# One block for the second and third feed-forward stage, the first head pair prepared early, and masks made in the first attention

## What is computed

```python
x = x + L0_xattn(layernorm(x), ctx)            # 16 heads of 16
x = x + L0_ffn(layernorm(x), w_gate, w_up, w_down)
x = x + L1_xattn(layernorm(x), ctx, mask, ...)  # 16 heads of 64, a null key and value
x = x + L1_ffn(layernorm(x), ...)              # 8 experts, the best two
```

```python
x = act_qdq(x)                      # scale = max|x| / 32767
up = act_qdq(x @ deq(w_up).T)
gate = act_qdq(x @ deq(w_gate).T)
sig = fixed_qdq_u16(sigmoid(gate))
gate = act_qdq(gate * sig)
o = act_qdq(gate * up)
return o @ deq(w_down).T
```

## Time and profile before

| what | value |
|---|---|
| median of three executions | 1203.74 us (1201.26 to 1206.43) |
| the profiled execution | 1201.73 us, span 1200.0 us |
| PE busy | 1092.3 us, 91% |
| DVE busy | 954.8 us, 80% |
| ACT busy | 602.0 us, 50% |
| POOL busy | 473.6 us, 39% |
| stage 2 of the feed-forward step | 384.2 to 482.0 |
| stage 3 | 482.0 to 566.9 |
| stage 4 | 566.9 to 644.7 |

### The profile page before, as it was taken

How to read it: one execution, slowest core, us unless ns; L and a number is a source line. 1 busy time by engine, 2 the same in 40 slices (tenths; PEclk the granted TensorE clock), 3 DMA queues, 4 the chain that set the end, 5 groups by cost and what they waited for, 6 DMA issues and landing times. The chain is left out here.

```text
span 1200.0 us, 19905 instructions
## 1 busy us (share of the span) xinstructions
PE 1092.3 (91%) x6208; PEld 902.4 (75%) x6208; DVE 954.8 (80%) x2563; ACT 602.0 (50%) x1337; POOL 473.6 (39%) x546
## 2 busy tenths in 40 slices
PE   7899999996898885895997899999999969999997
PEld 5677777885786664442996898889989858888786
DVE  4688998886685989897664888988888759888886
ACT  1566766773555887586781333433433323333332
POOL 1245445432000757674000444555554434343433
PEclk9899999998899998687898999999999979999999
DMA  9000000000233686597204011011000000000000
GB/s 275 1 2 1 1 1 1 1 2 1 106 119 127 220 291 245 162 350 266 88 1 144 21 44 45 1 45 45 1 1 1 1 1 19 18 17 17 26 18 26
DMA packets 50048, 82.56 MB, mean 69 GB/s; under 512 B 4636, under 2 KB 35696, under 8 KB 49968
## 3 DMA queue, kind: packets, MB, share of 16 engines
q1 hardware_dynamic: 48591, 80.77, 19.9%
q10 hardware_dynamic: 1376, 0.79, 0.3%
HBM read 45.65 MB, written 35.90 MB: 68 GB/s over the span
## 5 line engine op out<-in xcount | busy, mean ns | idle before, releaser
L1134 PE MATMUL a_ps<-VW,a_PT 128*128 128x256 f32 x640 | 143.5, 379 | 0.0
L1134 PEld LDWEIGHTS a_ps<-VW,a_PT 128*128 128x128 f32 x640 | 120.2, 190 | 15.0
L1172 ACT ACTIVATE a_U<-a_U 128x1280 f32<-128x1280 f32 x32 | 40.7, 1271 | 110.7 <-DVE a_U L1257 110.7
L2245 POOL TENSOR_TENSOR m_half<-m_half 128x512 f32<-128x512 f32 x32 | 41.2, 1286 | 130.6 <-ACT m_half L2207 130.6
L1151 ACT COPY a_PT<-a_ps 128x512 f32<-128x512 f32 (+1 forms) x96 | 46.0, 517 | 82.6 <-PE a_ps L1097 82.6
L2147 PE MATMUL m_ps<-m_wh,m_xh 128*128 128x512 f32 x256 | 86.6, 420 | 0.0
L915 DVE TENSOR_SCALAR a_U<-a_ps 128x320 f32<-128x320 f32 x128 | 59.2, 484 | 32.8 <-PE a_ps L723 21.5
L1850 POOL TENSOR_SCALAR f_sg<-f_sg 128x1024 f32<-128x1024 f32 x24 | 36.7, 1529 | 113.6 <-ACT f_sg L1807 113.2
L2147 PE MATMUL m_ps<-m_wl,m_xh 128*128 128x512 f32 x256 | 80.9, 398 | 0.0
L1249 DVE TENSOR_REDUCE a_mx<-a_ps 128x4 f32<-128x320 f32 x128 | 62.4, 488 | 22.8 <-PE a_ps L1084 22.4
L2147 PE MATMUL m_ps<-m_wh,m_xl 128*128 128x512 f32 x256 | 80.6, 396 | 0.0
(11 more groups left out here) (257 smaller groups left out, 3179.6 us busy)
## 6 DMA issues: line engine op xcount, KB each, us to landing
up_scratch<-f_ub SPq DMA_DIRECT2D x24, 512.0 KB, 3.0
f_ul<-up_scratch SPq DMA_DIRECT2D x24, 512.0 KB, 5.5
key_scratch<-p_keys SPq DMA_DIRECT2D x8, 640.0 KB, 6.7
vw_scratch<-p_vw SPq DMA_DIRECT2D x16, 320.0 KB, 5.7
k_raw<-key_scratch SPq DMA_DIRECT2D x8, 640.0 KB, 6.1
VW<-vw_scratch SPq DMA_DIRECT2D x4, 1280.0 KB, 5.7
xs<-in_x SPq DMA_DIRECT2D x4, 1024.0 KB, 12.4
h_scratch<-f_hh SPq DMA_DIRECT2D x8, 512.0 KB, 2.7
```

What stands on the lines that cost most here:

```text
L1134: last = pe.matmul(Y[:, 0:D], PTs[t.p][:, j, :], fold.values[t.batch % 2][:, j, :], start=(j == 0), stop=(j == NJ - 1))
```

## The change

- The blocks of stages 2 and 3 become one. On each engine the third stage's work follows the second's without a common end in between; the necessary waits are written out (ACT waits for `s_ua`, `s_uw` and `s_sc` before the first `ints`, POOL for `kup` alone).
- The first head pair is prepared at the end of stage 2: `mask_key(0)` in DVE's last chunk, then `mask_key(1)` and `mask_value(0)` ahead of the two maxima; on PE two query transposes, two key products, a value product and the four folded keys of pair 0 ahead of `rows_max(2)`. In stage 3 pair m now goes with units 3m-3 to 3m-1, and an iteration m = 8 has only units and the values of pair 7.
- `rows_max`, `fold_max`, `spread_max` and `integer_scale` use a list of banks `top`, and the column `2 * P` for the spread value. The last one lies in a bank that the value products do not use, and its wait for `s_We` is gone.
- `masks` moves to the first attention, behind body t = 28 on DVE (`MASKS = 28`), with its loads on SP behind the loads of x; the masks are stored to `mask_scratch` and read back as two contiguous tiles in `load_small`, which has six transfers instead of seven.
- The null value is no longer added from a tile of its own; POOL copies it to column `NKEY` of each sequence.
- `load_values` and `load_out` of the first two pairs leave chunks 2 and 3 and come between the first loads of up units behind the last store. The weight tiles are placed in other parts of the freed weights, so they can't be loaded before the last up product.

```diff
 class Prepare0:
+    def masks(self, dve):
+        dve.wait_ge(self.s_mk, 48)
+        dve.memset(mb[:], 0.0).then_inc(s_nv, 1)
+        dve.wait_ge(s_nv, 1)
+        dve.tensor_copy(mb[:, :, 0:NKEY], self.m8[:, :, 0:NKEY]).then_inc(s_nv, 1)
+        dve.wait_ge(s_nv, 2)
+        dve.tensor_scalar(nm[:], mb[:], -1.0, 1.0, ALU.mult, ALU.add).then_inc(s_nv, 1)
+        dve.tensor_reduce(nneg[:], mb[:, :, 0:NKEY], AX.X, ALU.add).then_inc(s_nv, 1)
+        dve.wait_ge(s_nv, 4)
+        dve.tensor_scalar(nm[:], nm[:], self.nk[:, 0:1], None, ALU.mult).then_inc(s_nv, 1)
+        dve.tensor_scalar(nneg[:], nneg[:], float(-NKEY), None, ALU.add).then_inc(s_nv, 1)
...
 # attention0, vector
+                    if t == MASKS:
+                        pr.masks(dve)
...
 # null_value, gpsimd
-        pool.tensor_tensor(self.VT[m % 2][:], self.VT[m % 2][:], self.nve[:].rearrange("p b k -> p (b k)"),
-                           ALU.add).then_inc(self.s_ve, 1)
+        pool.tensor_copy(self.VT[m % 2][:].rearrange("p (b k) -> p b k", b=B)[:, :, NKEY],
+                         self.nv[:, 0:1].broadcast_to([P, B])).then_inc(self.s_ve, 1)
...
 # ffn
+        top = [ps[6], ps[7], ps[6], ps[7], ps[0]]
...
 # tensor, behind the up products
+                pe.wait_ge(s_ue, MF * NCH)
+                p1.query_T(pe, 0, 0)
+                p1.query_T(pe, 0, 1)
+                p1.key_product(pe, 0)
+                p1.key_product(pe, 1)
+                p1.value_product(pe, 0)
+                folded(0)
                 rows_max(pe, 2)
                 rows_max(pe, 3)
                 spread_max(pe, 2)
                 spread_max(pe, 3)
+                for m in range(1, NM):
+                    p1.value_product(pe, m)
+                    if m + 1 < NM:
+                        p1.key_product(pe, m + 1)
+                    folded(m)
+                p1.folded_value(pe, NM - 1, 0)
+                p1.folded_value(pe, NM - 1, 1)
+                rows_max(pe, 4)
+                spread_max(pe, 4)
...
 # scalar
+                act.wait_ge(s_g2, NU)
+                for i in range(4):
+                    p1.key_out(act, 0, i)
...
+                act.wait_ge(s_sc, SCALED)
+                ints(0)
+                ints(1)
+                for m in range(1, NM + 1):
+                    if m < NM:
+                        p1.key_out(act, m, 0)
+                        p1.key_out(act, m, 1)
+                    ints(3 * m - 1)
+                    p1.value_out(act, m - 1, 0)
...
 # sync
                     if t.t0 in (2, 3):
                         p1.load_keys(sp, t.t0 - 2)
-                        p1.load_values(sp, t.t0 - 2)
-                        p1.load_out(sp, t.t0 - 2)
...
-                for i in range(4):
-                    load(sp, At(i))
+                p1.load_values(sp, 0)
+                load(sp, At(0))
+                p1.load_out(sp, 0)
+                load(sp, At(1))
+                p1.load_values(sp, 1)
+                load(sp, At(2))
+                p1.load_out(sp, 1)
+                load(sp, At(3))
+                p1.load_values(sp, 2)
+                p1.store_keys(sp, 0)
...
 # vector
+                        if t.t0 == NCH - 1 and q == 1:
+                            p1.mask_key(dve, 0)
                 pipeline(dve, body, 0, NCH - 1, 2, 5)
+                p1.mask_key(dve, 1)
+                p1.mask_value(dve, 0)
...
-                product(0)
-                p1.masks(dve)
-                p1.mask_key(dve, 0)
-                for m in range(NM):
-                    if m >= 1:
-                        product(3 * m)
-                    p1.mask_value(dve, m)
-                    product(3 * m + 1)
+                for m in range(1, NM + 1):
+                    product(3 * m - 3)
+                    if m < NM:
+                        p1.mask_value(dve, m)
+                    product(3 * m - 2)
                     if m + 1 < NM:
                         p1.mask_key(dve, m + 1)
-                    product(3 * m + 2)
+                    product(3 * m - 1)
```

More of the change, by code:

```diff
@@ L540, in query_T @@
             pe.wait_ge(self.s_wk[0], 32)
[L541 to L542 removed]
+        last = pe.transpose(self.query_bank(m, k), self.wq[m // 2 % 2][:, k, m % 2 * P:(m % 2 + 1) * P],
+                            self.ident[:])
         if m == 0:
@@ L1506, in ffn @@
     ROUND = 12582912.0
+    SCALED = 16
     def s(n):
@@ L1815, in _, with ints @@
                 pipeline(act, body, 0, NCH - 1, 2, 5)
+                p1.key_scale(act)
+                for k in range(KT):
+                    act.wait_ge(p1.s_T, k + 1)
+                    p1.query_out(act, 0, k)
+                act.wait_ge(s_g2, NU)
+                for i in range(4):
+                    p1.key_out(act, 0, i)
+                def ints(u):
+                    if u >= NU:
+                        return
+                    if u >= 2:
+                        act.wait_ge(s_pr, u - 1)
+                    act.activation(gq[u % 2][:], unit(u), ACT.Copy, scale=ksl).then_inc(s_g3, 1)
+                act.wait_ge(s_ua, NU)
+                for i in range(2):
+                    act.wait_ge(s_uw[i], 16 * NU // 2)
+                act.wait_ge(s_sc, SCALED)
[8 more added lines that the diff above has]
+                    if m < NM:
+                        p1.key_out(act, m, 2)
+                    ints(3 * m)
+                    if m < NM:
+                        p1.key_out(act, m, 3)
+                    p1.value_out(act, m - 1, 1)
+                    ints(3 * m + 1)
             @block.sync
@@ L1855, in _, with rounded @@
                     body(At(t))
+                def rounded(u):
+                    if u < NU:
+                        v = ul[u % 4][:]
+                        pool.wait_ge(s_ul[u % 4], 16 * (u // 4 + 1))
+                        pool.tensor_scalar(v, v, kup, ROUND, ALU.mult, ALU.add).then_inc(s_uq, 1)
+                p1.null_key(pool, 0)
+                p1.null_value(pool, 0)
+                p1.null_key(pool, 1)
+                pool.wait_ge(s_sc, SCALED - 4)
+                rounded(0)
+                rounded(1)
+                for m in range(1, NM + 1):
+                    rounded(3 * m - 1)
+                    if m < NM:
+                        p1.null_value(pool, m)
+                    rounded(3 * m)
+                    if m + 1 < NM:
+                        p1.null_key(pool, m + 1)
+                    rounded(3 * m + 1)
             @block.vector
```

239 lines of the change are left out of this document (86 added, 153 removed).

## The result

The changed kernel takes 1195.84 us (median of 20 runs, 1190.64 to 1204.79) where the kernel before takes 1204.72 on the same chip (20 runs, 1198.98 to 1210.26): a ratio of 0.9927, 95% interval 0.9910 to 0.9945, or 8.9 us less. The profiled execution of the changed kernel took 1196.02 us (span 1194.3), 5.7 less than that of before. So the forecast of 1196.8 holds for the total. Its parts don't all: two costs and one gain were taken too small, and another gain has the wrong cause.

What follows compares the result with a forecast made beforehand. It took DVE as the busiest engine that cannot overlap itself in stages 2 and 3. The terms +1.6 - 3.3 + 2.0 - 3.1 - 4.1 gave -6.9 us, a median of 1196.8 us, own range 1193.5 to 1200.

Steps and rivals of the forecast that it cites:

- part 3: Seam between stages 2 and 3: pair 0's work ahead of the maxima delays product 0, +2.0 us (+0.4 to +3.7).
- part 4: Stage 3 itself: DVE loses the mask work (1.9 us) and three of sixteen pair masks (1.2 us), -3.1 us.
- part 1: First attention: six mask instructions on DVE behind body t = 28 push the next clip, +1.6 us (0 to 2.3).
- The first attention's end at 298.6: Sign expected in the profile after: the first attention ends 1.6 us later, at 298.6.
- Part 2: Stage 2: fewer loads on SP ahead of the stores shorten DVE's three stalls, -3.3 us (0 to 5.2 gained).
- Rival (a): Stage 2's stores are limited by bytes, so fewer loads bring about 0: -3.6 in all, 1200.1 us; chance 16%.
- the slow end: Seam with PE at 1.2 GHz: folded keys end near 483.6, product 0 starts at 487.8, +3.7 us.
- rival (c): Stage 3: DVE's stalls on ACT go as well, up to -5.4 us, 1191.4 us; chance 16%.
- Part 5: Tail of stage 3: the 4.1 us in which the last maximum waits for PE's transpose go, -4.1 us.
- The rule: Against the change: PE work spread over the seam with gaps falls back to half rate, so more pairs would be slow.
- rival (d): PE stays at 1.2 GHz through the merged block, seven pairs slower: +14.7 us, 1211.5 us; chance 5%.

Runs made afterwards that it cites:

- e7: The changed kernel itself, not altered, measured as another sample: 1195.06 us, ratio 0.9915 to the kernel before.
- e5: The kernel before with the value and output weight loads of the first two pairs moved from stage 2 to behind the last store: 1203.74 us, ratio 0.9983.
- e9: The kernel before with the mask load and two key-null loads moved from stage 2's small batch to behind the last store: 1200.24 us, ratio 0.9954.
- e10: The changed kernel with the masks behind t = 29 and all of load_small ahead of chunk 0 of stage 2: 1191.97 us, ratio 0.9876.
- e4: The changed kernel with the null value again added over the whole tile by GpSimd, not copied to one column: 1194.87 us, ratio 0.9919.
- e1: The changed kernel with the six mask operations behind body t = 29 instead of t = 28: 1191.54 us (4 runs), ratio 0.9875.
- e2: The changed kernel with the maxima at the seam ahead of pair 0's folded products: 1195.83 us, ratio 0.9931 to the kernel before.
- e11: The kernel before with one matmul instead of two in each key and value product of the pairs: 1201.92 us, ratio 0.9967.
- e6: The kernel before with only the last max transpose given its own bank and its wait for pair 7's copies dropped: 1203.48 us, ratio 0.9985.

## Why the prediction was right, and where it was not

The sum was -6.9 us, the medians say -8.9 and the profiles -5.7. Stages 2 and 3 give -12.0 in the profiles, not -8.5; the first attention takes back more than 1.6. The total came nearer than its terms deserve: part 3 was short by 2.8 us as a loss and part 4 by 5.3 as a gain, and part 1 was short too. That these cancel is luck.

**Part 1** (+1.6). The push is right to a tenth: 1.54 us on the same instruction in all five profiles with the masks at 28. What failed is "I charge the whole 1.6 us" as the whole cost: the ratios of six kernels say about 5, with 4 either way, the profiles 2.5 on average. The first attention's end at 298.6 as the sign was a bad test, since that end moves by 9 us between executions of the same instructions.

**Part 2** (-3.3). U goes from 94.4 to 89.5 in the first profile and 91.4 in e7, so -3.0 to -4.9. The number is near, the mechanism was wrong: the working counted how long each load held SyncE, 0.8 us for the small batch and 1.3 for each pair of weight loads. e5 shows 0.6 us for all the weights, e9 4.1 us for three small loads. The time lay in the transfers behind the queue, a term that the working doesn't have. Only the third stall, 0.9 of its 1.17 us, went with the weight loads, as the working said. Rival (a), stores limited by their bytes, falls: in e9 the same bytes less 39 KB pass, and stage 2 is 4.1 us shorter.

**Part 3** (+2.0, ends +0.4 and +3.7). S went from 5.8 to 10.6, +4.8, in the profiles of the changed kernel, e7, e10 and e4: above the upper end. In e1 it is 8.0, since there the clock rose again before the folded keys. The clock was at 0.50 from 477 until product 0, so the slow end, +3.7, was the one to hold. Up to the value product it does: the working has key product 1 start 2.8 us ahead of VectorE's last unit's end and the value product end 1.5 us behind it, measured are 3.3 ahead and 1.4 behind. The 1.40 us that key product 1 waits for the mask of pair 0 are in the working. The step that failed is the folded keys, "to 483.6": 3.7 us for the four with their two transposes, by "two of the folded keys 1.44 us". In the trace they take 4.9 us, from 483.20 to 488.11, and so do the ones of the kernel before, in the lines behind that of the earlier trace rows:

```profile
491.24 0.47 PE L541 MATMUL f_ps<-ident,p_wq 128*128 128x128 f32 x1
491.64 1.43 PE L577 MATMUL f_ps<-p_k,p_wqT 64*128 64x320 f32 x2
493.01 0.47 PE L541 MATMUL f_ps<-ident,p_wq 128*128 128x128 f32 x1
493.41 1.43 PE L577 MATMUL f_ps<-p_k,p_wqT 64*128 64x320 f32 x2
```

Only the first two stand next to each other and take 1.44 us together; the other two have a transpose ahead of each and take 1.43 us each. These 1.2 us account for the 1.1 by which S exceeds the slow end (+4.8 against +3.7).

**Part 4** (-3.1). Q went from 75.9 to 67.5, and over all samples from about 76.4 to 68.0 (e1: 69.2): -8.4. The mask work and three pair masks are 3.1 of it. In the first two profiles the waits for ScalarE behind product 0 fell by 2.3 us (5.4 to 3.1), the products themselves by 3.2 (36.2 to 33.0); in the means over five profiles of the old form and four of the changed one, the waits by 3.1 (6.3 to 3.2) and the products by 1.9 (35.3 to 33.4). "The DVE stalls on ACT I leave" is the step that failed, and rival (c) names the reason in part: pair 0 is done ahead, and TensorE has seven pairs and not eight beside the 24 products. e2 shows it from the other side: with pair 0 back inside, Q is 72.6. e11 shows that TensorE's work sets part of VectorE's pace there. So parts 3 and 4 are one account, S + Q: 81.7 before (81.4 to 83.2 over five profiles), 77.2 to 78.4 with the changed kernels, 78.8 in e2, 80.0 in e4. The prediction gave -1.1 to the two, they bring about -4. The split of that -4 between stalls and faster products stays open: the two trade places from one profile to the next.

**Part 5** (-4.1). Right in size and cause; e6 leaves the shift as the cause, and the wait as nothing by itself.

**The rule** on the clock gate: rival (d) didn't occur. After, the clock is low from 477 to 494, partly around 516 and 526, and from 549 on; the first three pairs behind the seam took 8.2 to 8.4 us each, the next 10.0. That agrees in kind with the Trainium skill, "TensorE: Matmul & The Clock Gate", section "HAM oscillation — how this bites in real kernels" (TensorE's work broken up by waits falls back to half rate again and again), but the fall doesn't hold for whole pairs. And the clock sets more here than the chance of (d) tells: S is 2.6 us shorter in e1, whose clock is back at 2.4 GHz from the folded keys on, and it moves the end of the first attention.

## What to carry to other kernels

Before you charge a stalled store to the loads in front of it, count packets and look at GB/s in that stretch: a broadcast mask and two loads of four-byte columns cost 4.1 us where 448 KB of weights cost 0.6. Work put onto an engine is free or not by one place in its order: behind the body after which nothing of it is awaited the same six instructions cost nothing, one body earlier at least the 1.5 us of the wait, and some 5 us by the ratios. When a sum prices a group of instructions from one row, check that the others of the group stand as close together: two of the four folded keys didn't. When a stretch is moved ahead of a barrier, add the stretch before and the stretch behind into one account, since an engine that starts early only to wait for another gains nothing.

## What the runs showed of the hardware

TensorE's clock is low at different places in executions of the same instructions: in the first attention from 40 to 47 and from 286 to the end (end at 304.7), or from 15 to 28, from 274 to 278 and from 291 on (end at 296.9). Single profiles of this kernel therefore differ by up to 9 us in one stage with no cause in the code; a stage's gain has to be read in lengths that the clock doesn't touch, or over several profiles.

With some 630 more packets under 512 bytes, the 16 DMA engines moved 7 GB/s for about 4 us, in the kernel before:

```profile
412.00:416.00 4.00, 3.06 (x12) 2.18 (x12) 4.00 (x4) 2.04 (x2) 3.75 (x4) 1.00 0.08 7
```

The share of busy time there is 0.08: the engines count as idle, and yet the stores of 512 KB behind these packets wait. The Trainium skill, "DMA: Bandwidth & Descriptors", section "Specifications", asks for transfers of 512 bytes or more for the full rate. The trace agrees in kind (7 GB/s with them, 4.1 us less without), and shows what such packets cost those behind them.
